# New issue orders on five engines and a new table of PSUM banks, in a four-block transformer kernel on one Trainium2 core

## What is computed

```
x = x + 0.5 * ffn0(layernorm(x))      # silu(gate) * up, int weights minus 128, per-row scales
x = x +       attn0(layernorm(x))     # 16 heads of 16, rotary embedding, causal softmax
x = x + 0.5 * ffn0(layernorm(x))
x = x + 0.5 * ffn1(layernorm(x))      # sigmoid(x1) * x2, weights quantised to -1, 0, 1
x = x +       attn1(layernorm(x))     # 16 heads, 4 key/value heads, ALiBi, causal, + bias bo
x = x + 0.5 * ffn1(layernorm(x))
```

## Time and profile before

| what | value |
|---|---|
| median of 3 runs | 574.97 us (574.43 to 575.48) |
| the profiled execution | 575.79 us |
| its span, first to last instruction | 574.1 us |
| mean granted clock of TensorE, share of full | 0.988 |
| busy: TensorE / VectorE / ScalarE / GpSimd | 542.1 / 461.5 / 401.0 / 340.9 us |

### The profile page before, as it was taken

One profiled execution on the slowest core, in us unless ns is written; L12 is line 12 of the kernel. 1 busy time (PEld: TensorE's weight loads), 2 busy tenths in 40 slices (PEclk: granted clock), 3 DMA queues, 4 the chain that ended last, 5 costly groups with the idle time before them and its releaser, 6 DMA issues.

```text
span 574.1 us, 12962 instructions
## 1 busy us (share of the span) xinstructions
PE 542.1 (94%) x5060; PEld 303.2 (53%) x5060; DVE 461.5 (80%) x813; ACT 401.0 (70%) x605; POOL 340.9 (59%) x427
## 2 busy tenths in 40 slices
PE   8994998998998999999899999998999999999997
PEld 7462643544653654555446564465465645554664
DVE  4799789998989788499986879876898677784453
ACT  5895296688577768776596848857769686679534
POOL 2358699964997588856546365424372935445644
PEclk9998998999999999999999999998999999999999
DMA  8800021021021100230210120020201003011201
GB/s 328 322 2 1 2 102 46 21 76 41 21 96 56 40 1 2 90 109 2 71 32 19 41 71 21 3 60 0 70 24 46 14 23 107 23 39 41 77 37 38
DMA packets 20525, 31.76 MB, mean 55 GB/s; under 512 B 7360, under 2 KB 8768, under 8 KB 20312
## 3 DMA queue, kind: packets, MB, share of 16 engines
q1 hardware_dynamic: 20464, 30.94, 15.6%
HBM read 13.75 MB, written 2.36 MB: 28 GB/s over the span
## 4 chain that ended last, share of the span: by engine, by line
PE 61%; DVE 13%; ACT 7%; POOL 6%; issue 5%; DMA 4%; SPq 3%; DVEq 0%; POOLq 0%; ACTq 0%
PE PS L593 19%; PE PS L704 10%; PE PS L617 9%; PE PS L684 5%; PE PS L635 5%; PE PS L669 5%; PE PS L719 3%; DVE MX L1058 3%; ACT PB L846 3%; PE PS L577 2%; DMA MASKM<-maskm 2%; PE PS L651 2%; PE PS L541 2%; ACT XN L769 1%; POOL PB L1162 1%
## 5 line engine op out<-in xcount | busy, mean ns | idle before, releaser
L846 ACT ACTIVATE PB<-PS 128x1024 f32<-128x1024 f32 x160 | 157.6, 1023 | 41.8 <-PE PS L684 40.7
L1058 DVE TENSOR_REDUCE MX<-PS 128x2 f16<-128x1024 f32 (+2 forms) x192 | 157.6, 864 | 18.2 <-PE PS L541 17.7
L593 PE MATMUL PS<-XT,WGU 128*128 128x512 f16 x660 | 155.9, 380 | 2.7 <-DVE DS L1019 0.8
L1134 POOL TENSOR_TENSOR HH<-TH,HH 128x512 f16<-128x512 f32 x71 | 82.5, 1176 | 70.6 <-ACT HH L814 70.4
L1162 POOL TENSOR_SCALAR_AFFINE_SELECT PB<-PB 128x512 f32<-128x512 f32 (+1 forms) x140 | 73.1, 551 | 65.2 <-ACT PB L846 65.1
L593 PEld LDWEIGHTS PS<-XT,WGU 128*128 128x128 f16 x660 | 59.3, 98 | 76.2 <-issue 5.5
L617 PE MATMUL PS<-WD,HH 128*128 128x256 f16 x660 | 77.2, 273 | 0.8 <-POOL HH L1134 0.5
L704 PE MATMUL PS<-PB,V 128*32 128x512 f32 (+3 forms) x1024 | 75.6, 435 | 0.5 <-POOL PB L1162 0.4
L617 PEld LDWEIGHTS PS<-WD,HH 128*128 128x128 f16 x660 | 62.7, 98 | 12.7 <-issue 1.8
L669 PE MATMUL PS<-SK,SQ 63*128 63x256 f16 (+3 forms) x512 | 60.2, 302 | 6.3 <-DVE MX L1058 2.5
L814 ACT ACTIVATE HH<-TH 128x512 f16<-128x512 f32 (+1 forms) x86 | 51.6, 626 | 15.3 <-DVE TH L1001 8.5
(11 more groups left out here) (117 smaller groups left out, 781.2 us busy)
## 6 DMA issues: line engine op xcount, KB each, us to landing
SQ<-QPB SPq DMA_DIRECT2D x24, 256.0 KB, 2.5
...
SQ<-MT SPq DMA_DIRECT2D x128, 1.0 KB
...
```

Of the source, the lines that this page charges most:

```text
L593: m = e.matmul(o[:, :], WGU[l][:, k, col:col + P], rows_of(f)[j][:, k, :], start=j == 0 and k == 0, stop=j == 1 and k == 1)
L846: e.activation(PB[Q % 2][:, j, :, :], two_banks("s", i), ACT.Exp, scale=0.25).then_inc(a_exp, 1)
L1058: e.tensor_reduce(mx[:, :, pr, t], o[:, :, col:col + (t + 1) * P], AX.X, ALU.max, negate=True).then_inc(a_max, 1)
L1134: e.tensor_tensor(hh[1][:, s * T:(s + 1) * T], value_of(j)[0], hh[0][:, s * T:(s + 1) * T], ALU.subtract).then_inc(f_lo, 1)
```

## The change

Nothing but strings: `ORDER["sp"]`, `["pe"]`, `["dve"]`, `["act"]`, `["pool"]` and `["banks"]`. Every string holds the same steps the same number of times as before (106, 731, 530, 533 and 295), and there are 683 bank digits as before. No code, tile, wait or instruction is different. Where a step has moved, it has done so by up to 28 places, and mostly by one to four; in every part of the kernel there are such moves. The start of two of the strings:

```
     "pe":
-        "zzzzzzzzzzttzgggGGgGGggttzzaGggggGdddgdzzGGtatzgGGuuqqqddddvqgggggGGGGvuugGttqqzmmmggmmmmmqmsqssdmgG"
...
+        "zzzzzzzzzttzgggGgggGGGttzzGaggzzggGdddggdGztaGGztuuGqqqgggdddvdvqgGGGgGuugtGqqtzmmmgmmmgmmqmdqsmsgsG"
...
     "pool":
-        "wwwrrrhhhhhdhdrewwhhhhssadaqqdsesaaqqhssaawhhhhqqssfaafwfdqfqdffhhfefffffhcfffhhCcCssaaqfffrsqadsaqq"
...
+        "wwwrrhrhhhhwdwdherhhhshasqaddqessaaqqhhhssaahhqqwwssaaffqfdqfdfhffhefffhffhfffhccCCssaaqfffrqssdaaqq"
```

More of the change, by code:

```diff
@@ L108 @@
     "sp":
[L109 to L110 removed]
+        "kkrrkrkDrSrRDSRrrDkSkRrrDSRrrkDrSRkDSRlrkkrrrDSRrlDSRrkkrrDrSDRSrRrkkrDrDrSSRRrDrkkDrSSRRrOOrDrSRDSO"
+        "ROOOOO",
     "pe":
[L112 to L113 removed]
@@ new lines @@
+        "smdsmmdmsdmmspmssGmsgsmGsspsmgmsmGmmpsmsmsgssGmmmpsmsvsvmssmuummmpqqssoooossddmsqqmmmpttdsssdgmgggss"
+        "GGgmmpmssGmssmmgGsGmmpssmmvvsuuddmmsddssqqmmpoottssoogmssqgmggmGGGsgmspsmmgssGGqttpsssgdssdddpggGgGm"
+        "mgvgmmmvGuuGmmGooooqmsmqmssqmssdmmmdddsmmssssmmpmmmssttspgssmgGGgggsmmGGgGmsspsmdttdddmssggpmmmvgggu"
+        "usGGGssqmqmsgGmsqGoossmpmmddddmsmssoommpmttsssggGssGsgmmmpsgGmssgmmGGgmpsmsvsmsmmmdddmsdsspssmttoomm"
+        "gggsGuuooqqqGsmmsgmGGgsgGmspmmsdmmdssdsmdmsspmsmsmsmpssttvmmgGggGGgggsGGsmmssttddsddoooommmpspuugsmm"
@@ new lines @@
+        "qqsqssggsGGssspmsmgGmmmpmmvgmmtgGmssGsmstsmmpddddssmoomgoosssggmGmGsmmpmssgGssggssspssttGGpggGddddgg"
+        "GGggGGooooddddttgggGgGGgGGgdddd",
+    "dve":
+        "NwNtthhNhkhwwwttwhwhwwhhwwdNdwhwnwkhwuutthpqqhpwhdqdnpphqkhhhuuhtpqpqtmmmmmmxmssmmpqpqmhxhmdmmmsmmxd"
+        "mhkmshnmmxmsmmhmcmmxshmmmmcmxmuummmxpqpqooNdmqppmmqmttcdmsxhsskhhsmmnmmhmmxsshhmmmmcuxudmmdNppmqmqtt"
+        "ooNmxhmmhhpqkmhmmxhcpqhttsddhnksshchmmssmmmhuuxhmmsoohmmllmmxlmmdmdmmxNmmmmmxttNmhhckhmmhhhmmxttddmn"
+        "sshmmkmscuusxhhhmlmssmhlhlommxmddmNmmmomxttNhhmmhkmmhcxmmhhmmmcxmmmmddnmttmmosshxuusokhlllhmmmxshssh"
+        "hmmmmmxdmdmNmmmxmNcttmmchhhkhhhmmxttddnoommmNuuhmmxlllhhckmmhmmmmxmmmhmchmxmmttddmmohoxNmmhhmmmxkhch"
+        "tthhhcddkhhhhooNXttddhhkhhhhdd",
@@ new lines @@
+    "act":
+        "TwwXxxwttthwhtXthhxxtkktthhwXwwtwhhkkkttYtyyxxhhhXhtttQhvQwwwvkktYtyyQtQxhhhxhhtTQQkteeeeQtQeeehhoee"
+        "eteeheeotehYoeeeteehhoeeevveeyycceoeeQeeQXoxxeeeQtQttheethhoteeeehteYoeehhcvvyyeeeecXoxxeeeeQQttthXh"
+        "heettheoteexhxQhoeeeeetQhotthttvYchvyychhthQeQeeQeeeeeeeoXexxeeotetehhtthteXthhheeoxxeeettohYvttcyye"
+        "eehhQtetQcehhQeheoeeeXxxeeoetteeethhheoteeXhtthhoeeveeeceecoexexYttteyyhQQQheehttethehhoeeeeeeoeeeXo"
+        "exxveXttthhhtttheheheexxcceYeooyytehQQeeeQtteeeeoetXohhhvtteeeeehhxxcoceeteeehttXhheoeeteeteeeeeoxxh"
+        "thohttchhtthtchthhXxxthtthththhth",
@@ L139 @@
+        "ffrhfffhhhhccCCeffffhhhhhffbddfffrrhhhhhccCCffeffrffbfffhhhhhccCCfrffhhffffffhhhcChchChhhrhhhhh",
     "banks":
[L140 to L143 removed]
@@ new lines @@
+        "6206240612652046230437402642014634056215260470636501624604621460321670426704127517620564620563506215"
+        "0264036402406304612460242065062047620740265675240623406420427163406230460253476057620526207502412064"
+        "3063562406260360246054702607240725426056241063046204620461244262406730462705431632704261470526742162"
+        "4146420462460264026056240164137250147251624063214051624061345026450204360456024602540265024560425620"
+        "56205620726204720162401264702462461042672046043205172164536427140514603073260476501",
```

37 lines of the change are left out of this document (5 added, 32 removed).

## The result

The changed kernel takes 564.99 us, median of six executions (563.99 to 568.08), beside 575.23 us of the kernel before on the same chip (574.21 to 578.08). The ratio is 0.983, 95% interval 0.980 to 0.987: 10.2 us less, where 5.0 were forecast. The profiled execution took 565.08 us, span 563.3.

The account below looks back on a forecast made before the run. VectorE's queue, held up by GpSimd, was taken to set the first attention unit's start. 4.60 + 0.46 = 5.06, say 5.0 us, off the profiled 575.79 gives 570.8; 0.8 above the median, so 570.0 us, range 567.0 to 574.2.

Parts of the forecast that it names:

- the sum on VectorE up to the first m reduction: VectorE from about 44 us: 2.35 quantisation + 3.00 two waits - 0.75 longer wait = 4.60 us, reduction at about 83.3, not 87.91.
- the term for the rest: 98.5 to 574 us: neighbour swaps only, 16.95 us of idle in pieces too small to name, taken as 0.
- the m stretch: From 87.08 us on TensorE: reductions still set the pace, only the first s step's wait goes, 0.46 us.
- The bound and the mechanism: Front: VectorE's queue sets the first m step; GpSimd's WA subtraction collides with L960 and moves ahead at no cost.
- The quantisation: VectorE's two w1/w2 halves: 4.0 and 6.0 us, 10.0 instead of 12.35, saving 2.35 us (0 to 4.40).
- Rival A: Second quantisation half: the lock only moves, four waits of 1.27 us, 8.13 us instead of 6.0; total 572.8, 0.17 with Rival D.
- The waits: VectorE: 1.53 and 1.47 us before shuffles go, saving 3.00; the second unit's statistics wait grows from 0.61 to 1.35, -0.75 us.
- The low clock in the front: TensorE, first projection to first m: 3.60 us at low clock, alone 1.8 us; TensorE follows with 2 us over.
- The first s step: After the m reductions on TensorE: its 0.46 us wait for its row of maxima goes, behind a d and a q step.
- Rival C: After 98.5 us: one idle piece in seven or one later clock dip goes, about 2.5 us more, 567.5; chance 0.12.
- Rival B: Attention part: closer bank hand-overs bring twelve more waits for exp, 4.8 us, 7 with p steps; 577, chance 0.13.
- Rival D: Front: TensorE's down projection waits over 2 us for low halves, clock falls again; inside Rival A's time, 0.17 together.

## Why the prediction was too small

Two steps of the prediction failed. The first is the sum on VectorE up to the first m reduction: 4.60 us forecast, 6.52 measured. The second is the term for the rest, put at 0: it measured 3.8. On TensorE that makes 6.18 us at the first m step, 0.8 in the m stretch (forecast 0.46) and 3.8 behind it, 10.8 between the two spans, where 5.06 was forecast.

- **The bound and the mechanism** held. VectorE's queue set the front, the two engines collided at L960, WA's subtraction fits at 34 us for nothing, and moving it alone gives half of the result. In the changed kernel VectorE no longer binds alone at the end of the front: the first m step waits 0.71 us for the transfer of SK, and VectorE then waits 0.40 us for TensorE.
- **The quantisation was mis-sized.** Forecast 4.0 + 6.0 us, a saving of 2.35; measured 2.8 + 6.0, a saving of 3.5. The second half was right. Of the 1.2 us missed in the first, 0.25 is that 3.05 adds up four durations whose records overlap: undisturbed, the half takes 2.8 us, as in the run with GpSimd's move alone, where GpSimd stood idle beside it. The other 0.95 is that I let eight tiny steps of GpSimd hold VectorE up, and it was they that gave way. L1113 took 1.70 us beside L964, and L1125 1.49 us just ahead of the quantisation beside L1009, against 1.04 for either elsewhere in the trace. The Trainium skill, "SBUF — State Buffer", section "SBUF: two separate sides", says that the loser blocks until the winner's instruction ends. The 0.66 us are less than one L964 (0.94) and the 0.45 less than that L1009 (0.69), so both agree with a wait for the rest of one; no run here tests it alone. Rival A, four waits of 1.27 us in the second half, didn't come: 6.0, not 8.1. That is 0.8 us for each of the four instructions, and GpSimd's steps beside them took 1.44 to 1.92 us instead of 1.15 to 1.27, so there both engines paid.
- **The waits** were booked too high, 3.00 - 0.75 = 2.25 us. The three named are at 0, 0 and 0.73 us, but 1.03 and 1.48 came in new places. All of VectorE's waits from the quantisation to the first m reduction were 5.1 us and are 4.4: 0.7 saved. 
- **The account began too late.** The quantisation starts 1.6 us sooner in the changed kernel (45.99, not 47.58), and one L1009 of 0.7 us is done ahead of it instead of behind. I had not followed the strings ahead of 44 us. With the quantisation (3.5) and the waits (0.7): 3.5 + 0.7 + 1.6 + 0.7 = 6.5 at the first m reduction (81.39 for 87.91) where 4.6 was forecast.
- **The low clock in the front** was judged by TensorE's reserve alone (2 us over). It also reached VectorE through the late projection: in the run with the warming steps VectorE waits 1.27 us less before the first shuffle, and the first m step comes 1.1 us sooner, which is little more than the 0.9 by which two traces can differ.
- **The first s step** was to give 0.46. Its wait is gone, but a d and a q step now stand ahead of it, and the gain there is 5.69, less than at the first m. Both orders meet again at the first p step: 7.00. So this stretch gave 0.8.
- **"The rest: 0"** was the second step that failed. From the first m step to the end it was 487.0 us and is 482.4, outside the 2 us that I had allowed. 0.8 is the stretch just named and 0.3 lies up to 385 us. The other 3.5 lie between 385 and 404: 1.7 the low clock of that one execution, which a repeat hasn't, and 1.5 to 1.8 the wait for OT. That wait was there to be read in the kernel before as one piece, and I had called the pieces too small to name:

```profile
PE PS L577 <- ACT OT L856: 1.5, 1, 1.5
```

  Rival C named both kinds of source at 2.5 us and 0.12; that the profiled execution's own clock was part of my base is what I missed. No reading of the strings foretold the end of the wait either, since what makes the transfer late is open: this part of the gain is found and not explained.
- **Rival B**, the attention part pays by closer bank hand-overs, didn't come: waits for exp on L669 fell from 2.4 us in six pieces to 1.5 in four. Those on L684 rose from 1.5 us in four to 2.7 in five, so the two together went from 3.9 us in ten pieces to 4.2 in nine, far from twelve more. **Rival D** neither: the down projection starts at 57.0 and the clock stays full.
